# Second attention phase of a four-phase transformer kernel: regrouping DMAs two at a position, row transfers on ScalarE's queue

## The chip, the cores and the metric

The kernel runs on one core of a Trainium2 chip. The metric is the device time of one execution in microseconds (us), the median of several runs.

## What is computed

The input x (4 batches of 512 tokens, 512 features) goes through four residual blocks: causal attention with grouped keys and rotary embedding, a feed-forward block with 4-bit weights, causal attention with 32 heads and biases, and the feed-forward block again.

```python
x = x + _L0_attn_a_ref(_layernorm(x, axis=-1), ...)
x = x + _L0_ffn_ref(_layernorm(x, axis=-1), ...)
x = x + _L0_attn_b_ref(_layernorm(x, axis=-1), ...)
x = x + _L0_ffn_ref(_layernorm(x, axis=-1), ...)
```

The change touches the third block, which is

```python
q = (x @ Wq.T + bq).reshape(b, l, h, hd).transpose(0, 2, 1, 3)
...
scores = jnp.einsum('bhqd,bhkd->bhqk', q, k) / math.sqrt(hd)
...
att = jax.nn.softmax(scores, axis=-1)
out = jnp.einsum('bhqk,bhkd->bhqd', att, v)
out = out.transpose(0, 2, 1, 3).reshape(b, l, d)
return out @ Wo.T + bo
```

with h = 32 heads of hd = 16 and l = 512 tokens per batch.

## The kernel before, in words

The four phases run one after the other; tiles of the second attention phase have names that begin with `ab_`, those of the first with `aa_`. Each engine has its own instruction queue, written out by the same walk over positions; semaphores tie the queues together.

A batch is 16 pairs of heads, s = 0 to 15, and each pair has SUB = 5 positions, i = 0 to 4, so that a batch has positions 0 to 79. At every position TensorE makes one chunk of 512 columns of transposed scores (`exp_scores`, L1122), ScalarE takes its exponential (L834), GpSimd cuts off what lies above the diagonal (L691). Score banks alternate between two. At the same position TensorE makes score blocks of a pair two ahead, from which VectorE finds row maxima (`max_scores` L1082 and L1083, `reduce_max` L945 to L949). At i = 4 of an even pair the values matmuls (L1142) of the two pairs before follow.

The maximum is subtracted inside the score matmul: three more rows of the operand hold it, split into bf16 parts. For each pair they go from GpSimd's split through a transpose (L1106, i = 2 of the pair before) to VectorE's copy into `rowparts` (L958) and then by a DMA, the row transfer (L605), into the stacks. The first score chunk of a pair waits for it (`rows_made`).

The stacks hold Q and K of eight heads (a unit, four pairs) as rows of bf16 parts, in two buffers that alternate by unit. For each unit there is one projection of Q and one of K (tasks "Q" and "K", L247 with 12 matmuls and one for the bias). ScalarE, VectorE and GpSimd split the result into a high, middle and low part (`parted`, L810, L1024, L839, L716), and twelve DMAs of 128 KB, the sends, regroup them by head into the stacks (`regroup`, L652). The maxima of a unit's first pair wait for all twelve (`stacked`), and they begin two pairs ahead: unit u = 2 (pairs 8 to 11), for instance, is first read at position 30, in pair 6. The buffer that its sends overwrite is last read by the scores of position 19.

Other TensorE work stands at positions that a table, PLAN_B, sets: V (projection of values, positions 5 to 11), F and C (transposes of the context), O (output projection of the batch before, 14 to 17), X (transposes of the next batch's normalised x, 46, 48, 53, 56). Their results go through two task banks in PSUM. Q stands at 0, 20, 40 and 60, K two positions later, the last pair of them for the next batch. Only pairs 0 to 3 of the first batch and the end of the last run outside that rhythm: the last batch has no X and no Q and K for a next one.

Everything DMA in this phase is issued by SyncE, in order of position: the row transfer at i = 2, then the sends of Q and K two and three positions after their projection, loads of x, residuals, stores. The row transfer waits there for VectorE's copy, the sends for the parts:

```python
                        if i == ROWS_AT and (after := following(region, b0 + bs, s, 1)) is not None:
                            max_rows(*after)
                    for kind, bb, u, _ in table.started(region, pos, 2, "Q", "K"):
                        regroup(b0 + bb, u, QK.index(kind), (0,))
```

Of the kernel before, what the change touches and what calls it, by code (L numbers as in the profile page):

```python
# [250 lines left out]
class Timetable:  # L251
# [36 lines left out]
    def names(self, region):  # L288

        out = []  # L290
        for pos in range(len(region[0])):
            out += [(kind, u, t, 0) for kind, _, u, t in region[1].get(pos, []) if kind != "T"]
            out += [("T", u, t, p) for _, u, t, p in self.turned(region, pos)]
        return out
# [67 lines left out]
def attention(nc, phase, name, consts, x_dram, y_dram, w_dram, kv_heads, units, plan, head,  # L362
# [28 lines left out]
    with ExitStack() as ctx:  # L391
# [149 lines left out]
        SLOTS = (((0, 1, 2), (3, 4), (5,)), ((2, 4, 5), (0, 3), (1,)))  # L541
# [19 lines left out]
        block = ctx.enter_context(nc.Block())  # L561

# [8 lines left out]
        def _(sp):  # L571
# [29 lines left out]
            def max_rows(b, s):  # L601

                sp.wait_ge(rows_copied.sem, rows_copied.at(b, s + 1))
                h, _, _ = heads(s, 0)
                sp.dma_start(stacks[MAXROW:MAXROW + 3, unit(s) % 2, h:h + 2, :],  # L605
                             rowparts[MAXROW:MAXROW + 24, :]).then_inc(rows_made.sem, 16)

# [10 lines left out]
            def part(region, where, b0):  # L618
                for pos, step in enumerate(region[0]):
                    if step is not None:  # L620
                        bs, s, i = step
                        if i == ROWS_AT and (after := following(region, b0 + bs, s, 1)) is not None:
                            max_rows(*after)
                    for kind, bb, u, _ in table.started(region, pos, 2, "Q", "K"):
                        regroup(b0 + bb, u, QK.index(kind), (0,))
                    for kind, bb, u, _ in table.started(region, pos, 3, "Q", "K"):
                        regroup(b0 + bb, u, QK.index(kind), (1, 2))
# [14 lines left out]
                    if step is None and region is table.head and region[0][pos + 1] is not None:  # L642
                        max_rows(0, 0)

            def regroup(b, u, a, parts):

                for c in parts:
                    made, n = ((high_made, 1), (middle_made, 1), (lowest_made, 1))[c]
                    sp.wait_ge(made.sem, made.at(b, 2 * u + a + n))
                    for slot in SLOTS[a][c]:  # L650
                        first = HU if a else 0
                        sp.dma_start(stacks[slot * HD:(slot + 1) * HD, u % 2, first:first + HU, :],  # L652
                                     parted[:, a, c, :])\
                          .then_inc(regrouped[a].sem, 16)
# [90 lines left out]
        def _(act):  # L745
# [33 lines left out]
            def part(region, where, b0):  # L779
                for pos, step in enumerate(region[0]):  # L780
# [939 lines left out]
def late(first, step, kind):  # L1720
# [13 lines left out]
)  # L1734
PLAN_B = timed(
    *[(20 * (u - 1) + j, kind, 0, u, 0) for u in range(1, 4) for kind, j in (("Q", 0), ("K", 2))],
# [4 lines left out]
    *[(60 + j, kind, 1, 0, 0) for kind, j in (("Q", 0), ("K", 2))],  # L1741
# [75 lines left out]
```

## Time and profile before

| what | value |
|---|---|
| median of 3 runs | 1956.14 us (1955.39 to 1958.18) |
| the profiled execution | 1951.68 us, its span 1949.9 us |
| mean granted TensorE clock | 0.929 of full speed |
| busy: PE (TensorE), DVE (VectorE), ACT (ScalarE), POOL (GpSimd) | 1658.7, 1099.6, 861.1, 650.3 us |
| second attention phase, scores | from 987 to 1577 us of the span |

The span is cut by phase: the first attention phase ends near 576 us, the first feed-forward phase near 925 us. In a row of the timeline the first number is the start, the second the time until the last instruction of the row ended, and the bracket holds the engine's idle time before the row and what ended it. SPq is SyncE's queue; PEld is the weight load of TensorE.

### The profile page before, as it was taken

Reading aid. Unit: us, or ns where it says so; the run is one execution under the profiler, and the core shown is the slowest. Engines: PE = TensorE matmul, PEld = TensorE weight load, DVE = VectorE, ACT = ScalarE, POOL = GpSimd, SP = SyncE. Lnnn points to the kernel's source line nnn. Section 1 sums busy time; section 2 is a strip of 40 time slices with the busy share of each in tenths; the row PEclk is TensorE's granted clock in tenths of the full one; section 3 lists DMA queues with packets and bytes.
Section 4 is the critical chain, followed back from the end, with each engine's and each line's share of the span. In section 5 each row is a group of like instructions: output and inputs, shape, how many; then the busy total and the mean of one; then the engine's idle time right before and its main releaser. Section 6 shows DMA issues by size and latency. Waiting matters only on the chain. (4 is left out here: it accounts for less than half of the span.)

```text
span 1949.9 us, 31436 instructions
## 1 busy us (share of the span) xinstructions
PE 1658.7 (85%) x10544; PEld 1157.8 (59%) x10544; DVE 1099.6 (56%) x2394; ACT 861.1 (44%) x1514; POOL 650.3 (33%) x1926
## 2 busy tenths in 40 slices
PE   4888988989857999998288798798888857999997
PEld 4555655656535787786155475465555435777785
DVE  5777676676627654543555645644644527654543
ACT  3456555565524544532334433443443425454541
POOL 4455455454421221311224433433432412221211
PEclk8899999999997999999589898999889988999999
DMA  2000000001016311010534433633453226311010
GB/s 99 2 20 17 34 24 24 24 2 34 13 56 187 94 60 65 0 44 22 154 38 54 68 60 52 87 45 66 59 64 66 35 69 181 92 54 65 0 44 22
DMA packets 78118, 106.95 MB, mean 55 GB/s; under 512 B 13194, under 2 KB 49674, under 8 KB 77972
## 3 DMA queue, kind: packets, MB, share of 16 engines
q1 hardware_dynamic: 77972, 105.10, 24.1%
q8 instruction: 80, 1.31, 0.3%
q14 instruction: 66, 0.54, 0.1%
HBM read 62.34 MB, written 16.78 MB: 41 GB/s over the span
## 5 line engine op out<-in xcount | busy, mean ns | idle before, releaser
L247 PE MATMUL f_ring<-f_xt,f_codes 128*128 128x512 f32 (+1 forms) x1408 | 360.6, 399 | 6.6 <-DVEq L1539 5.5
L247 PEld LDWEIGHTS f_ring<-f_xt,f_codes 128*128 128x128 f32 (+1 forms) x1408 | 263.7, 188 | 76.0 <-DVEq L1539 6.2
L1397 POOL TENSOR_TENSOR f_ht<-f_work,f_ht 128x512 fp32r<-128x512 f32 (+1 forms) x88 | 114.6, 1306 | 472.9 <-ACT f_ht L1457 472.9
L834 ACT ACTIVATE ab_region<-ab_scores 128x512 f32<-128x512 f32 x320 | 181.0, 600 | 144.3 <-PE ab_scores L1122 144.2
L691 POOL TENSOR_SCALAR_AFFINE_SELECT ab_region<-ab_region 128x128 f32<-128x128 f32 x512 | 140.3, 298 | 240.5 <-ACT ab_region L834 240.2
L834 ACT ACTIVATE aa_region<-aa_scores 128x512 f32<-128x512 f32 x320 | 184.5, 599 | 81.3 <-PE aa_scores L1122 78.5
L1550 DVE TENSOR_TENSOR f_work<-f_ring,f_work 128x512 f32<-128x512 f32 (+1 forms) x176 | 120.6, 689 | 146.1 <-ACT f_work L1446 117.3
L1446 ACT ACTIVATE f_work<-f_ring,f_scales 128x512 f32<-128x512 f32 (+1 forms) x176 | 120.8, 686 | 171.7 <-PE f_ring L247 171.3
L1122 PE MATMUL ab_scores<-ab_stacks 99*128 99x512 bf16 (+3 forms) x512 | 135.4, 328 | 69.8 <-DMA ab_stacks<-ab_rowparts 66.8
L247 PE MATMUL f_ring<-f_dcodes,f_ht 128*128 128x512 f32 (+1 forms) x704 | 176.0, 404 | 10.3 <-DVE f_down_x L1520 9.3
L691 POOL TENSOR_SCALAR_AFFINE_SELECT aa_region<-aa_region 128x128 f32<-128x128 f32 x512 | 137.6, 299 | 88.5 <-ACT aa_region L834 88.0
L247 PEld LDWEIGHTS f_ring<-f_dcodes,f_ht 128*128 128x128 f32 (+1 forms) x704 | 133.0, 192 | 48.4 <-DVE f_down_x L1520 12.9
L1082 PE MATMUL aa_maxima<-aa_stacks 96*128 96x128 bf16 (+3 forms) x512 | 142.4, 312 | 21.4 <-DVE aa_nmax L949 15.6
L1082 PE MATMUL ab_maxima<-ab_stacks 96*128 96x128 bf16 (+3 forms) x512 | 147.6, 328 | 13.0 <-issue 12.6
L949 DVE TENSOR_REDUCE ab_nmax<-ab_maxima 128x1 f32<-128x384 f32 (+1 forms) x256 | 148.4, 616 | 17.6 <-PE ab_maxima L1083 14.9
L949 DVE TENSOR_REDUCE aa_nmax<-aa_maxima 128x1 f32<-128x384 f32 (+1 forms) x256 | 146.1, 614 | 2.7 <-PE aa_maxima L1083 1.0
L1122 PE MATMUL aa_scores<-aa_stacks 99*128 99x512 bf16 (+3 forms) x512 | 125.3, 306 | 7.2 <-DMA aa_stacks<-aa_rowparts 3.6
L1083 PE MATMUL ab_maxima<-mask_qk,identb 128*128 128x128 bf16 x512 | 115.4, 236 | 0.0
L1122 PEld LDWEIGHTS ab_scores<-ab_stacks 99*128 99x128 bf16 x512 | 45.6, 105 | 109.3 <-issue 84.7
L1083 PE MATMUL aa_maxima<-mask_qk,identb 128*128 128x128 bf16 x512 | 109.6, 226 | 0.0
L247 PE MATMUL ab_tasks<-ab_xt,ab_w 128*128 128x512 f32 x384 | 97.6, 403 | 7.0 <-DVE ab_bias L876 7.0
L945 DVE TENSOR_REDUCE ab_nmax<-ab_maxima 128x1 f32<-128x128 f32 x128 | 36.5, 285 | 117.1 <-PE ab_maxima L1083 117.1
(181 smaller groups left out, 2962.2 us busy)
## 6 DMA issues: line engine op xcount, KB each, us to landing
ab_stacks<-ab_parted SPq DMA_DIRECT2D x192, 128.0 KB, 5.6
f_x<-mid SPq DMA_DIRECT2D x32, 256.0 KB, 4.2
f_raw<-mid SPq DMA_DIRECT2D x32, 256.0 KB, 4.2
f_raw<-in_gate_q SPq DMA_DIRECT2D x10, 512.0 KB, 6.6
f_raw<-in_up_q SPq DMA_DIRECT2D x10, 512.0 KB, 4.9
f_raw<-in_down_q SPq DMA_DIRECT2D x10, 512.0 KB, 3.7
aa_x<-in_x SPq DMA_DIRECT2D x16, 256.0 KB, 2.8
aa_res<-in_x SPq DMA_DIRECT2D x16, 256.0 KB, 2.7
```

The source lines that it names most:

```text
L247: mm = pe.matmul(out, w, x, start=start and i == 0, stop=stop and i == len(pairs) - 1)
L691: last = pool.affine_select(out=chunk[:, at:at + P], in_=chunk[:, at:at + P], compare_op=ALU.is_ge, fill=0.0, base=0, pattern=[[1, P]], ch ...
L834: act.activation(probs[:, s // 2 % 2, SUB * (s % 2) + i, :], scores[:, sbk, :], ACT.Exp, scale=0.25).then_inc(scores_freed[sbk].sem, 1)
L945: dve.tensor_reduce(nm[:, h, 0:1], src[:, 0:P], AX_X, ALU.max, negate=True)
L949: last = dve.tensor_reduce(nm[:, h, qt:qt + 1], src[:, 0:(qt + 1) * P], AX_X, ALU.max, negate=True)
L1082: pe.matmul(out, lhs, rhs, start=True, stop=False, skip_group_check=True)
L1083: return pe.matmul(out[:, diag:diag + P], identb[:], mask[:], start=False, stop=True, skip_group_check=True)
L1122: mm = pe.matmul(scores[:, sbk, at:at + n], st[:, hk, kb * P:(kb + 1) * P], st[:, h, kb * P:T], start=True, stop=True)
L1397: pool.tensor_tensor(ht[0:r, LO, n, :], hid[0:r, n % 2, :], ht[0:r, HI, n, :].bitcast(F32), ALU.subtract).then_inc(hid_lo.sem, 1)
L1446: act.activation(scaled[0:r, j, :], src, ACT.Identity, scale=scales[0:r, j, n:n + 1])\
L1550: dve.tensor_tensor(dst, src, scaled[0:r, j, :], ALU.add)\
```

## The change

Three things change in the second attention phase; the first phase keeps its row transfers on SyncE (`if rope`).

1. The row transfer is issued by ScalarE's queue, behind the exponential of i = 3, the fourth of a pair.
2. The twelve sends of a unit are tasks of the plan ("S", numbers 0 to 11), two at a position: at positions 20, 21, 23, 24, 25 and 26 for unit 2, likewise from 40 and 60, and at 2, 3, 4, 5, 6 and 8 for unit 1. Ahead of the two, SyncE waits until the score chunk of the position before is made (`scores_seen`).
3. Q of units 2, 3 and of the next batch's unit 0 is projected at 17, 38 and 58 instead of 20, 40 and 60, K at 20, 40 and 60 instead of 22, 42 and 62.

```diff
+        SENDS = ((0, 0, 0), (0, 0, 1), (0, 0, 2), (0, 1, 3), (0, 1, 4), (1, 0, 2), (1, 0, 4), (1, 0, 5), (0, 2, 5),
+                 (1, 1, 0), (1, 1, 3), (1, 2, 1))
...
+        def max_rows(eng, b, s):
+
+            eng.wait_ge(rows_copied.sem, rows_copied.at(b, s + 1))
+            h, _, _ = heads(s, 0)
+            eng.dma_start(stacks[MAXROW:MAXROW + 3, unit(s) % 2, h:h + 2, :],
+                         rowparts[MAXROW:MAXROW + 24, :]).then_inc(rows_made.sem, 16)
...
-                        if i == ROWS_AT and (after := following(region, b0 + bs, s, 1)) is not None:
-                            max_rows(*after)
-                    for kind, bb, u, _ in table.started(region, pos, 2, "Q", "K"):
-                        regroup(b0 + bb, u, QK.index(kind), (0,))
-                    for kind, bb, u, _ in table.started(region, pos, 3, "Q", "K"):
-                        regroup(b0 + bb, u, QK.index(kind), (1, 2))
+                        if rope and i == ROWS_AT and (after := following(region, b0 + bs, s, 1)) is not None:
+                            max_rows(sp, *after)
...
+                    for n, (_, bb, u, t) in enumerate(table.started(region, pos, 0, "S")):
+                        if n == 0:
+                            scores_seen(b0 + bs, SUB * s + i - 1)
+                        regroup(b0 + bb, u, *SENDS[t])
...
+            def scores_seen(b, c):
+
+                sp.wait_ge(scores_filled[c % 2].sem, scores_filled[c % 2].at(b, c // 2 + 1))
+
+            def regroup(b, u, a, c, slot):
+
+                made = (high_made, middle_made, lowest_made)[c]
+                sp.wait_ge(made.sem, made.at(b, 2 * u + a + 1))
+                first = HU if a else 0
+                sp.dma_start(stacks[slot * HD:(slot + 1) * HD, u % 2, first:first + HU, :], parted[:, a, c, :])\
+                  .then_inc(regrouped[a].sem, 16)
...
                         act.activation(probs[:, s // 2 % 2, SUB * (s % 2) + i, :], scores[:, sbk, :], ACT.Exp,
                                        scale=0.25).then_inc(scores_freed[sbk].sem, 1)
+                        if not rope and i == ROWS_AT + 1 and (after := following(region, b, s, 1)) is not None:
+                            max_rows(act, *after)
...
+SENT = (0, 0, 1, 1, 3, 3, 4, 4, 5, 5, 6, 6)
```

SyncE's queue before, from pair 4 of the third batch on. A row with x12 is one unit's sends; rowparts rows are row transfers:

```order
L605 DMA ab_stacks<-ab_rowparts 3x8x128
L652 DMA ab_stacks<-ab_parted 16x8x512 x12
L605 DMA ab_stacks<-ab_rowparts 3x8x128 x4
L652 DMA ab_stacks<-ab_parted 16x8x512 x12
L605 DMA ab_stacks<-ab_rowparts 3x8x128
L578 DMA ab_x<-mid 128x512 x2
L605 DMA ab_stacks<-ab_rowparts 3x8x128 x3
L652 DMA ab_stacks<-ab_parted 16x8x512 x12
```

The same stretch of SyncE's queue in the changed kernel, from the last residual and stores ahead of it on:

```order
L612 DMA ab_res<-mid 128x512
L617 DMA mid<-ab_res 128x512
L612 DMA ab_res<-mid 128x512
L617 DMA mid<-ab_res 128x512
L660 DMA ab_stacks<-ab_parted 16x8x512 x24
L586 DMA ab_x<-mid 128x512 x2
L660 DMA ab_stacks<-ab_parted 16x8x512 x24
```

The row transfers are gone from it, and the sends of two units stand next to each other with nothing between them but their waits.

ScalarE's queue before, from pair 3 to pair 6 of the third batch. `ab_region<-ab_scores` is an exponential, `ab_parted` the casts of Q's and K's parts, `ab_avs` the copy of the context:

```order
L834 ACTIVATE ab_region<-ab_scores 128x512 x6
L810 CAST ab_parted<-ab_tasks 128x512
L834 ACTIVATE ab_region<-ab_scores 128x512 x2
L839 CAST ab_parted<-ab_rest 128x512
L810 CAST ab_parted<-ab_tasks 128x512
L834 ACTIVATE ab_region<-ab_scores 128x512 x2
L839 CAST ab_parted<-ab_rest 128x512
L777 COPY ab_avs<-ab_av 128x512
L834 ACTIVATE ab_region<-ab_scores 128x512 x9
L805 CAST ab_ct<-ab_tasks 128x512
L834 ACTIVATE ab_region<-ab_scores 128x512
```

And in the changed kernel, pairs 4 to 6 of the third batch:

```order
L841 ACTIVATE ab_region<-ab_scores 128x512
L817 CAST ab_parted<-ab_tasks 128x512
L841 ACTIVATE ab_region<-ab_scores 128x512 x2
L848 CAST ab_parted<-ab_rest 128x512
L841 ACTIVATE ab_region<-ab_scores 128x512
L568 DMA ab_stacks<-ab_rowparts 3x8x128
L841 ACTIVATE ab_region<-ab_scores 128x512
L784 COPY ab_avs<-ab_av 128x512
L841 ACTIVATE ab_region<-ab_scores 128x512 x4
L568 DMA ab_stacks<-ab_rowparts 3x8x128
L841 ACTIVATE ab_region<-ab_scores 128x512 x5
L568 DMA ab_stacks<-ab_rowparts 3x8x128
L812 CAST ab_ct<-ab_tasks 128x512
```

A row transfer stands behind each fourth exponential, ahead of the fifth; the casts keep their places behind the projections.

TensorE's queue before, from position 17 of pair 3 in the third batch to the end of that pair. The 12 matmuls from `ab_w,ab_ct` are O; `ab_scores` at 128x384 and 128x128 is the fourth chunk, at 128x256 x2 the fifth:

```order
L1150 MATMUL ab_tasks<-identf,ab_avs 128x128 x4
L247 MATMUL ab_tasks<-ab_w,ab_ct 128x512 x12
L247 MATMUL ab_tasks<-ab_bias,ab_sel 128x512
L1122 MATMUL ab_scores<-ab_stacks 128x384
L1122 MATMUL ab_scores<-ab_stacks 128x128
L1082 MATMUL ab_maxima<-ab_stacks 128x384
L1083 MATMUL ab_maxima<-mask_qk,identb 128x128
L1122 MATMUL ab_scores<-ab_stacks 128x256 x2
L1082 MATMUL ab_maxima<-ab_stacks 128x512
```

And in the changed kernel:

```order
L1159 MATMUL ab_tasks<-identf,ab_avs 128x128 x4
L247 MATMUL ab_tasks<-ab_w,ab_ct 128x512 x12
L247 MATMUL ab_tasks<-ab_bias,ab_sel 128x512
L247 MATMUL ab_tasks<-ab_xt,ab_w 128x512 x12
L247 MATMUL ab_tasks<-ab_sel,ab_bias_qk 128x512
L1131 MATMUL ab_scores<-ab_stacks 128x384
L1131 MATMUL ab_scores<-ab_stacks 128x128
L1091 MATMUL ab_maxima<-ab_stacks 128x384
L1092 MATMUL ab_maxima<-mask_qk,identb 128x128
L1131 MATMUL ab_scores<-ab_stacks 128x256 x2
```

The projection of Q (`ab_xt,ab_w`), which stood at position 20 behind this stretch, now stands behind O, ahead of the fourth chunk; behind the fourth chunk nothing but maxima and the fifth chunk is left in this pair.

## Rows read from the trace of the kernel before

**Rows 1.** Page: TensorE's busy time; the sends' size and time to landing.

```profile
PE 1658.7 (85%) x10544; PEld 1157.8 (59%) x10544; DVE 1099.6 (56%) x2394; ACT 861.1 (44%) x1514; POOL 650.3 (33%) x1926
...
ab_stacks<-ab_parted SPq DMA_DIRECT2D x192, 128.0 KB, 5.6
```

**Rows 2.** Windows, third batch and phase: busy us by engine, PEclk, DMA share, GB/s

```profile
1282.00:1436.00 154.00, 133.30 (x941) 86.47 (x942) 81.49 (x197) 63.08 (x116) 57.88 (x204) 0.91 0.42 60
...
sum 592.00, PE 507.25 PEld 325.16 DVE 308.54 ACT 248.02 POOL 226.44; mean PE 101.45 PEld 65.03 DVE 61.71 ACT 49.60 POOL 45.29
```

**Rows 3.** Waits of TensorE, 985 to 1577 us: total, times, longest.

```profile
PE ab_scores L1122 <- DMA ab_stacks<-ab_rowparts: 66.8, 24, 7.2
PE ab_tasks L1161 <- DVE ab_x L900: 10.5, 10, 2.1
```

**Rows 4.** Timeline of TensorE: first score chunks ahead of which it stood.

```profile
1079.40 0.58 PE L1122 MATMUL ab_scores<-ab_stacks 99*128 99x512 bf16 x1 [2.98 <-DMA ab_stacks<-ab_rowparts]
...
1232.56 0.58 PE L1122 MATMUL ab_scores<-ab_stacks 99*128 99x512 bf16 x1 [2.70 <-DMA ab_stacks<-ab_rowparts]
...
1269.18 0.58 PE L1122 MATMUL ab_scores<-ab_stacks 99*128 99x512 bf16 x1 [7.24 <-DMA ab_stacks<-ab_rowparts]
...
1353.66 0.59 PE L1122 MATMUL ab_scores<-ab_stacks 99*128 99x512 bf16 x1 [6.78 <-DMA ab_stacks<-ab_rowparts]
...
1387.31 0.58 PE L1122 MATMUL ab_scores<-ab_stacks 99*128 99x512 bf16 x1 [1.88 <-DMA ab_stacks<-ab_rowparts]
...
1540.80 0.58 PE L1122 MATMUL ab_scores<-ab_stacks 99*128 99x512 bf16 x1 [6.62 <-DMA ab_stacks<-ab_rowparts]
```

**Rows 5.** Timeline: SyncE's queue and VectorE's copy, pairs 4 and 5, third batch.

```profile
1338.37 7.76 SPq L652 DMA_DIRECT2D ab_stacks<-ab_parted  x12
...
1344.97 0.23 DVE L958 COPY ab_rowparts<-ab_av 24x128 bf16<-24x128 bf16 x1
...
1346.17 0.75 SPq L605 DMA_DIRECT2D ab_stacks<-ab_rowparts  x1
```

**Rows 6.** Line L652 from 1331 us (durations in ns); the window of their packets.

```profile
L652 SPq DMA_DIRECT2D ab_stacks<-ab_parted x12: 596/608/616, 1338.4 to 1345.5; - x12
...
1339.30:1352.20 12.90, 7.49 (x73) 3.88 (x71) 6.53 (x15) 5.33 (x10) 5.83 (x21) 0.94 1.04 123
```

**Rows 7.** Timeline: end of pair 7 of the third batch, start of pair 8.

```profile
1363.27 0.70 SPq L605 DMA_DIRECT2D ab_stacks<-ab_rowparts  x1
...
1363.55 0.38 PE L1122 MATMUL ab_scores<-ab_stacks 99*128 99x384 bf16 x2
...
1363.97 1.08 ACT L834 ACTIVATE ab_region<-ab_scores 128x512 f32<-128x512 f32 x2 [0.55 <-PE ab_scores L1122]
...
1364.71 0.22 PE L1083 MATMUL ab_maxima<-mask_qk,identb 128*128 128x128 bf16 x1
...
1365.30 0.38 PE L1122 MATMUL ab_scores<-ab_stacks 99*128 99x512 bf16 x1 [0.37 <-DMA ab_stacks<-ab_rowparts]
```

**Rows 8.** Timeline: pair 4 of the third batch.

```profile
1332.17 2.98 PE L247 MATMUL ab_tasks<-ab_xt,ab_w 128*128 128x512 f32 x12
...
1339.47 0.39 PE L1122 MATMUL ab_scores<-ab_stacks 99*128 99x384 bf16 x2
...
1340.15 1.09 ACT L834 ACTIVATE ab_region<-ab_scores 128x512 f32<-128x512 f32 x2
...
1343.08 0.39 PE L1122 MATMUL ab_scores<-ab_stacks 99*128 99x512 bf16 x1
```

**Rows 9.** Timeline: fourth chunk of pair 3, first chunk of pair 4, third batch.

```profile
1330.47 0.39 PE L1122 MATMUL ab_scores<-ab_stacks 99*128 99x384 bf16 x2
...
1331.70 0.38 PE L1122 MATMUL ab_scores<-ab_stacks 99*128 99x512 bf16 x1
```

**Rows 10.** Windows: the last of twelve stretches at half the clock, and their sum.

```profile
1565.70:1569.10 3.40, 3.40 (x16) 1.41 (x20) 0.92 (x2) 1.69 (x3) 2.19 (x9) 0.50 0.28 86
sum 92.40, PE 60.49 PEld 36.45 DVE 36.30 ACT 31.45 POOL 24.85; mean PE 5.04 PEld 3.04 DVE 3.02 ACT 2.62 POOL 2.07
```

More of the change, by code:

```diff
@@ L291, in names @@
         for pos in range(len(region[0])):
-            out += [(kind, u, t, 0) for kind, _, u, t in region[1].get(pos, []) if kind != "T"]
+            out += [(kind, u, t, 0) for kind, _, u, t in region[1].get(pos, []) if kind not in "TS"]
             out += [("T", u, t, p) for _, u, t, p in self.turned(region, pos)]
@@ L538, in attention @@
         OTHER_W = [max(head_at("P")) + 2 + 2 * f for f in range(KD)] if rope else [12, 13, 15, 16]
-        SLOTS = (((0, 1, 2), (3, 4), (5,)), ((2, 4, 5), (0, 3), (1,)))
+        SENDS = ((0, 0, 0), (0, 0, 1), (0, 0, 2), (0, 1, 3), (0, 1, 4), (1, 0, 2), (1, 0, 4), (1, 0, 5), (0, 2, 5),
+                 (1, 1, 0), (1, 1, 3), (1, 2, 1))
         FIRST = sum(len(ks) for ahead, ks in MAXIMA_AT if ahead == 2)
@@ L599, in _ @@
                 load(1, t)
[L601 to L606, printed above, removed]
             def residual(b, t):
@@ L621, in part @@
                         bs, s, i = step
-                        if i == ROWS_AT and (after := following(region, b0 + bs, s, 1)) is not None:
-                            max_rows(*after)
-                    for kind, bb, u, _ in table.started(region, pos, 2, "Q", "K"):
-                        regroup(b0 + bb, u, QK.index(kind), (0,))
-                    for kind, bb, u, _ in table.started(region, pos, 3, "Q", "K"):
-                        regroup(b0 + bb, u, QK.index(kind), (1, 2))
+                        if rope and i == ROWS_AT and (after := following(region, b0 + bs, s, 1)) is not None:
+                            max_rows(sp, *after)
+                    if step is None and region is table.head:
+                        for kind, bb, u, _ in table.started(region, pos, 2, "Q", "K"):
+                            for a, c, slot in SENDS:
+                                if a == QK.index(kind):
+                                    regroup(b0 + bb, u, a, c, slot)
+                    for n, (_, bb, u, t) in enumerate(table.started(region, pos, 0, "S")):
+                        if n == 0:
+                            scores_seen(b0 + bs, SUB * s + i - 1)
+                        regroup(b0 + bb, u, *SENDS[t])
                     for _, bb, _, t in table.started(region, pos, 2, "X"):
@@ L642, in part @@
                     if step is None and region is table.head and region[0][pos + 1] is not None:
[L643 to L654, printed above, removed]
+                        max_rows(sp, 0, 0)
+            def scores_seen(b, c):
[6 more added lines that the diff above has]
+                  .then_inc(regrouped[a].sem, 16)
             whole(sp, part)
@@ L1734 @@
 )
+SENT = (0, 0, 1, 1, 3, 3, 4, 4, 5, 5, 6, 6)
 PLAN_B = timed(
-    *[(20 * (u - 1) + j, kind, 0, u, 0) for u in range(1, 4) for kind, j in (("Q", 0), ("K", 2))],
+    (0, "Q", 0, 1, 0), (2, "K", 0, 1, 0),
+    *[(j, "S", 0, 1, n) for n, j in enumerate((2, 2, 3, 3, 4, 4, 5, 5, 6, 6, 8, 8))],
+    *[(20 * (u - 1) + j, "S", 0, u, n) for u in (2, 3) for n, j in enumerate(SENT)],
     *[(j, "V", 0, 0, t) for t, j in enumerate((5, 7, 9, 11))],
@@ L1740 @@
     *[(j, "X", 1, 0, t) for t, j in enumerate((46, 48, 53, 56))],
-    *[(60 + j, kind, 1, 0, 0) for kind, j in (("Q", 0), ("K", 2))],
+    (17, "Q", 0, 2, 0), (20, "K", 0, 2, 0), (38, "Q", 0, 3, 0), (40, "K", 0, 3, 0),
+    (58, "Q", 1, 0, 0), (60, "K", 1, 0, 0),
+    *[(60 + j, "S", 1, 0, n) for n, j in enumerate(SENT)],
 )
```

## The prediction

> **What bounds the kernel now.** I read the page first, to see which engine is full in the phase that the diff touches. TensorE is busy 85% of the span [rows 1]. Then I cut the second attention phase into its batches: in the third TensorE is busy 133.3 of 154 us (87%) at a mean granted clock of 0.91, VectorE, the next in busy time, 81.5 us (53%) [rows 2]. So what can be won is TensorE's idle time and its slow stretches. The waits of TensorE in this phase say who ends the idle time: 66.8 us in 24 waits end with the row transfer (ab_rowparts to ab_stacks); the next item, waits for the normalised x, is 10.5 us [rows 3].
>
> The 24 are of two kinds. Below, T4 is the start of pair 4's first score matmul, counted within a batch; positions run from 0 (pair 0, i=0) to 79. Seven long waits stand ahead of pair 6 (all batches) and pair 14 (not in the last batch, which regroups nothing there); one of 6.78 and the longest, 7.24, are shown. Four stand ahead of pair 10: 2.98, 2.70, 1.88 and 6.62 us, 14.2 together [rows 4]. Thirteen of about 0.37 us (4.8 together) stand ahead of pairs that follow a pair without a task behind its third score chunk, like the one ahead of 1365.30 [rows 7]. The seven are then 66.8 - 14.2 - 4.8 = 47.8 us.
>
> Why 6.8 us? SyncE's own queue tells it: twelve regrouping DMAs (third batch, pair 4 on) hold the queue from 1338.37 to 1346.13, and pair 6's row transfer starts only at 1346.17, though VectorE's copy was ready at 1345.20 [rows 5]. It then stands behind twelve times 128 KB [rows 1, 5]. During 12.9 us the DMA engines are full (share 1.04), so one regrouping DMA costs 12.9/12 = 1.07 us of them [rows 6]. TensorE resumes at 1353.66 [rows 4], 1.4 us after their end and 7.5 us after the row transfer's issue, where an undisturbed row transfer takes 2.03 us: issued 1363.27, next pair begins 1365.30 [rows 7].
>
> Removing the row wait alone would therefore give nothing: pair 6's first maxima need the regrouped stacks (the wait in `stacked`), which land at that same time. What counts is when the twelve sends land, and how much TensorE work lies before.
>
> **The change, part by part.** Times are against the profiled execution (1951.68 us, span 1949.9), which is 4.5 us under the median of 1956.14; I apply the difference to both.
>
> *Projections earlier, sends from position 20, 40, 60.* The projection of Q for the next unit moves from position 20 to 17 (40 to 38, 60 to 58), and K from 22 to 20. Work is the same: a projection is 2.98 us of matmuls and one for the bias, together about 3.1 us of TensorE [rows 8]. Before, pair 6 began 22.0 us after T4 (1331.70 [rows 9] to 1353.66). Afterwards pair 4 holds one projection less: 11.4 us (1331.70 to 1343.08 [rows 8]) - 3.1 = 8.3. Pair 5 has 3.8 us of work (1343.08 to the start of the wait, 1353.66 - 6.78 = 1346.88). So pair 6 could begin at T4 + 12.1. The sends: four go out at once (T4 to T4+2.5, 0.61 us of queue each [rows 6]); the next need the scores of positions 22 to 25, which follow K, so two each from T4+4.4, 5.4 and 6.0, and the last pair at T5+0.4 = T4+8.7, ending its issue near T4+10. Eight DMAs from T4+5.4 on keep the DMA engines to about T4+13.9, plus 1.4 for the tail as above: landed at T4+15.3. TensorE still does pair 6's first score chunk (0.2), then waits with the maxima: 15.3 - 12.1 - 0.2 = 3.0 us, at pair 14 likewise. Gain: 47.8 - 7 x 3.0 = 26.8 us. In the last batch pair 9 holds no transposes of x, and pair 10 behaves like pair 6: 6.62 - 3.0 = 3.6. In the first three batches pair 9 is long (about 8.7 us), the sends land before pair 10, and 2.98 + 2.70 + 1.88 = 7.6 is gained; the waits for normalised x (10.5 us in ten [rows 3]) stay. Sum of this part: 38.0 us.
>
> Q at positions 38 and 58 stands behind the fourth score chunk, so it also covers the row transfer of the short pairs 7 and 11: seven waits of 0.36 like that of [rows 7], 2.5 us gained. Moving K and Q past F, O and X costs nothing in work; the two task banks must be free for F, O and Q at position 17, but O's 3.1 us lie between F and Q.
>
> *Row transfer behind the fourth exponential, on ScalarE.* This is the price. VectorE's copy is at i=2; SyncE issued at once. In the short pair 7 the fourth chunk of scores starts at 1363.55, its exponential at 1363.97 and ends at about 1364.5, and TensorE could begin the next pair at 1364.93 [rows 7]. So the issue comes 0.7 to 1.3 us later than 1363.27, depending on whether ScalarE's queue issues while the exponential runs or after it. No DMA of ScalarE is in this trace. I take the later end and the 2.03 us measured on SyncE's queue: issue 1.05 after the chunk, 3.1 to the next pair, where 1.38 is work (1363.55 to 1364.93): a pause of 1.7 us instead of 0.37. Who pays: the short pairs without Q, V, X or values behind the fourth chunk. Pair 15 into the next batch (3 x 1.3 = 3.9). Pair 3, where the exponential also waits for the cast of Q now made at position 17: in the present trace such an exponential starts 0.68 instead of 0.42 after its chunk (1339.47 to 1340.15 [rows 8]). There the next pair starts 1.23 after the chunk today (1330.47 to 1331.70 [rows 9]) and would start at 3.3: 2.1 us, in four batches, less the 0.4 already paid in the first: 8.0. In the last batch pairs 11 and 13 (no Q): 2.6. Pairs 5, 9 of the last batch and 13 pay it inside the pause computed above. Sum: 14.5 us lost.
>
> Even pairs end with the values matmuls: from fourth chunk to next pair they need 3.6 us (1339.47 to 1343.08 [rows 8]) against 3.1, so they just hide it. But pairs 0 and 8 now have sends in flight at that moment; their packets share the DMA engines. Bounds: nothing, if the small packets slip between, to 1 us; I take 0.5 in eight cases, 4 us (pairs 4 and 12 absorb it in the later pause).
>
> The 0.70 us that the DMA takes on the issuing queue [rows 7] now falls on ScalarE, 63 times, 44 us, beside 248 us of work in the phase's 592 [rows 2]. It delays the fifth exponential, needed only by the second chunk of the next pair, which starts 0.5 us after the late first: covered. Without that cover it would be 0.7 us a pair.
>
> The Trainium skill (DMA: Bandwidth & Descriptors, Issuing engines are not separate DMA queues) says that DMAs of any engine run on the same 16 DMA engines, and issuing from several saves only the issue time. By that alone, a second queue would not shorten the wait behind sends; the full share in [rows 6] agrees that the engines are the shared resource. The same page (Queues, rings and completion order) has each DMA engine alternate between the queues that have work, which would let a small transfer slip in; no row here shows either. What the first reading would cost is rival 2, worked out from rows.
>
> *Clock.* After each long pause TensorE's granted clock is 0.5, the 1.2 GHz level, and a score matmul takes 0.58 [rows 4] instead of 0.38 us [rows 7]. Over the phase I count twelve such stretches, 60.5 us of TensorE busy in them [rows 10], so about 30 us are lost to half speed, 2.5 each. Shorter pauses may remove some; the nine new ones of 1.7 to 2.1 may each bring one like that at 1565.7, 3.4 us busy [rows 10], 1.7 lost, 15 in all. I take zero, with -15 and +30 as bounds.
>
> **Sum:** 38.0 + 2.5 - 14.5 - 4 = 22.0 us faster: 1929.7 for a profiled run, 1934 for the median.
>
> **Rivals.**
> 1. *The slow stretches go* as well, because no pause exceeds 3 us. For: a 0.37 us pause never has one behind it. Against: the pauses at pair 10 are 1.9 to 3 and have one. Half to two thirds of the 30: about 1916. Chance 0.20.
> 2. *Slower: row transfers still stand behind the sends.* Pair 4's rows are issued at T4+6.2 with about three sends' worth of backlog; if they wait for it, pair 5 begins at T4+10.7 instead of 8.3. In fifteen regroupings that is 15 x 2.4 = 36 us, 32 over what is counted: 1934 + 32 = 1966. It decides the sign from (22 + 4)/15 = 1.7 us a regrouping on. For: pair 6's 7.5 us today. Against: that was one queue, in order. Chance 0.07.
> 3. *A DMA on ScalarE's queue costs about 0.9 us more to land*: then four even pairs a batch and the short ones are exposed by it, about 25 times 0.9, which eats the 22: 1956, no change. Nothing in the trace shows or excludes it. Chance 0.08.
> 4. *The new pauses each bring a slow stretch*: 15 us back, 1949. Chance 0.15.
> 5. The forecast: 1926 to 1942, chance 0.50.
>
> The range runs from 1912 to 1955. What a measurement can tell from no change is 0.2%, 4 us. Cases 1, 4 and 5 give 0.85 for faster, of which I move 0.02 for misjudged tails: faster 0.83, same 0.07, slower 0.10.
>
> **What would show it.** Right: waits of scores for the row transfer ahead of pair 6 gone, and a wait of maxima on the regrouped stacks of about 3 us in its place; row waits of 1.5 to 2 us ahead of pairs 4 and 0; none ahead of pairs 8 and 12; ScalarE's row transfer starting as the fourth exponential ends. The step that I trust least is landing at T4+15.3: two us either way are 16 us in the sum. It would be wrong altogether if the row transfer lands later than 3 us after issue in most pairs, or if slow stretches of the clock grow in number.

## The result: about 10 us faster, where 22 were forecast

The changed kernel takes 1948.6 us (median of 10 runs, 1942.78 to 1952.22); the kernel before, run beside it, 1958.32 us (10 runs, 1955.39 to 1963.33). The ratio is 0.9946, 95% interval [0.9934, 0.9959]: faster by 0.4 to 0.7%. The profiled execution took 1948.8 us, its span is 1947.0 us, the mean granted clock 0.935.

The page of the changed kernel, TensorE's row and that of the sends (issue to landing in the last number, 4.1 us where [rows 1] has 5.6):

```profile
PE 1669.1 (86%) x10544; PEld 1159.5 (60%) x10544; DVE 1099.4 (56%) x2394; ACT 864.5 (44%) x1514; POOL 647.5 (33%) x1926
...
ab_stacks<-ab_parted SPq DMA_DIRECT2D x192, 128.0 KB, 4.1
```

From the first score of the phase to the first of its last pair the kernel before needed 583.26 us and the changed one 574.36, so the phase is 8.9 us shorter. The spans of the two traces differ by only 2.9 us, because outside the phase, where the change has next to nothing to act on, this trace of the kernel before is the quickest of all (1366.6 us against 1372.6, and 1370.0 to 1377.4 in the runs below). A difference of phases is therefore read from one trace each: run 8, which takes as long as the changed kernel, has a phase 2.7 us shorter. What TensorE waited for from 985 to 1577 us (total, times, longest), to be read against [rows 3]:

```profile
PE ab_scores L1131 <- DMA ab_stacks<-ab_rowparts: 45.5, 33, 3.3
PE ab_tasks L1170 <- DVE ab_x L909: 10.6, 9, 2.1
PE ab_av L1115 <- POOL ab_nparts L688: 6.2, 4, 2.3
PE ab_maxima L1091 <- DVE ab_nmax L958: 4.4, 11, 0.4
PE ab_maxima L1091 <- DVE ab_nmax L955: 3.6, 7, 0.5
```

The row waits fell from 66.8 to 45.5 us, 21.3 less. The third to fifth row show what ate almost half of that. Before, waits for GpSimd's parts were 1.6 us and those of maxima for VectorE 0.4 us. Now they are 3.9 and 8.1, 10.1 more. (The 6.2 of the third row hold one of 2.3 us ahead of the phase's first score; the kernel before has the same one, just outside the window.)

The row waits have also moved. By pair, over the four batches:

| wait ahead of pair | before, us each | changed, us each |
|---|---|---|
| 0 | 0.4 | 1.1 |
| 1 | 0 | 3.3 in the first batch, then 1.0 |
| 4 | 0.4 in the first batch, then 0 | 1.1 |
| 5 | 0 | 1.2 |
| 6 | 6.8 to 6.9 | 1.7 to 1.8 |
| 8 and 12 | 0.3 to 0.4 | 0 (12 in the last batch: 1.1) |
| 9 | 0 | 1.7 to 1.8 (0.8 in the first batch) |
| 10 | 3.0, 2.7, 1.9, 6.6 | 0.5, 0, 0.5, 2.7 |
| 13 | 0 | 0.6, 1.7, 0, 0 |
| 14 | 6.4 to 7.2 (0.4 in the last batch) | 1.3 to 2.7 (1.1 in the last batch) |

Two pairs of the third batch show how it goes. First the timeline from the fourth chunk of pair 3 (where [rows 9] stood), then that of pair 4's own transfer. ACTq is ScalarE's queue, SPq SyncE's; L568 is the row transfer:

```profile
1332.15 0.39 PE L1131 MATMUL ab_scores<-ab_stacks 99*128 99x384 bf16 x2
...
1332.59 0.73 ACTq L568 DMA_DIRECT2D ab_stacks<-ab_rowparts  x1
...
1332.83 1.14 ACT L841 ACTIVATE ab_region<-ab_scores 128x512 f32<-128x512 f32 x2
...
1333.02 13.71 SPq L660 DMA_DIRECT2D ab_stacks<-ab_parted  x12
...
1334.68 0.38 PE L1131 MATMUL ab_scores<-ab_stacks 99*128 99x512 bf16 x1 [1.14 <-DMA ab_stacks<-ab_rowparts]
...
1340.36 0.23 DVE L967 COPY ab_rowparts<-ab_av 24x128 bf16<-24x128 bf16 x1
1340.39 0.62 ACT L841 ACTIVATE ab_region<-ab_scores 128x512 f32<-128x512 f32 x1
...
1340.62 0.73 ACTq L568 DMA_DIRECT2D ab_stacks<-ab_rowparts  x1
...
1341.23 0.39 PE L1091 MATMUL ab_maxima<-ab_stacks 96*128 96x512 bf16 x1 [0.40 <-DVE ab_nmax L958]
...
1345.13 0.38 PE L1131 MATMUL ab_scores<-ab_stacks 99*128 99x512 bf16 x1 [1.17 <-DMA ab_stacks<-ab_rowparts]
```

Three things are to be seen. The issue at 1332.59 comes before the fourth exponential starts (1332.83), and the one at 1340.62 in the middle of one that lasts until 1341.01: ScalarE's queue issues the DMA without waiting for that exponential to end. With no send ahead of it the transfer takes 2.09 us (1332.59 to 1334.68), as on SyncE's queue [rows 7]. With sends in flight it takes 4.51 us (1340.62 to 1345.13), and TensorE stands 1.17 us ahead of pair 5.

The windows of pairs 4, 5 and 6 of that batch (length; busy us of PE, PEld, DVE, ACT and POOL with their instructions; PEclk, DMA share, GB/s):

```profile
1334.68:1345.13 10.45, 8.88 (x70) 4.84 (x71) 4.98 (x12) 4.36 (x8) 6.18 (x20) 1.00 0.65 111
1345.13:1350.39 5.26, 3.60 (x29) 2.27 (x30) 4.19 (x11) 2.87 (x5) 1.74 (x7) 1.00 0.53 75
1350.39:1357.81 7.42, 7.42 (x61) 3.98 (x62) 4.38 (x10) 3.36 (x6) 3.15 (x14) 0.77 0.00 1
```

Pairs 4 and 5 now take 15.7 us, where T4+15.3 was forecast: the end is nearly right, but it is reached in another way. Pair 4 takes 10.45 instead of 8.3 us, and the pause ahead of pair 6 is 1.7 instead of 3.0. The DMA engines are idle in pair 6: the sends had landed by then, and no maxima wait on them. In pairs 8 and 9 the pause that goes (the one ahead of pair 10) was only 1.9 to 3.0 us long in the first three batches [rows 4], and the slower pairs 8 and 9 eat more than that: over the four batches they lose 2.8 us, with the projection that left pair 8 put back. Pair 8 takes 11.6 us in the third batch:

```profile
1370.80 0.39 PE L1091 MATMUL ab_maxima<-ab_stacks 96*128 96x512 bf16 x1 [0.52 <-DVE ab_nmax L955]
...
1371.03 0.73 ACTq L568 DMA_DIRECT2D ab_stacks<-ab_rowparts  x1
...
1371.65 0.39 PE L1091 MATMUL ab_maxima<-ab_stacks 96*128 96x512 bf16 x1 [0.40 <-DVE ab_nmax L958]
...
1376.08 0.38 PE L1131 MATMUL ab_scores<-ab_stacks 99*128 99x512 bf16 x1 [1.71 <-DMA ab_stacks<-ab_rowparts]
```

That is 0.92 us of waits for VectorE within the pair and 1.71 behind a row transfer that took 5.05 us.

### The profile page after: what moved, and what is told of

Its sections match the earlier page's. It is cut to its first block and busy times, and to the rows that moved or that the text cites. A ratio compares the mean times of both kernels' runs of the same rounds, so it can differ in the third digit from the quotient of the medians.

```text
span 1947.0 us, 31527 instructions
## 1 busy us (share of the span) xinstructions
PE 1669.1 (86%) x10544; PEld 1159.5 (60%) x10544; DVE 1099.4 (56%) x2394; ACT 864.5 (44%) x1514; POOL 647.5 (33%) x1926
## 3 DMA queue, kind: packets, MB, share of 16 engines
q8 instruction: 80, 1.31, 0.3%
## 5 line engine op out<-in xcount | busy, mean ns | idle before, releaser
L1131 PE MATMUL ab_scores<-ab_stacks 99*128 99x512 bf16 (+3 forms) x512 | 130.1, 318 | 47.8 <-DMA ab_stacks<-ab_rowparts 45.5
```

The lines of the kernel that those rows point to most:

```text
L1131: mm = pe.matmul(scores[:, sbk, at:at + n], st[:, hk, kb * P:(kb + 1) * P], st[:, h, kb * P:T], start=True, stop=True)
```

## Experiments

All times are medians, all ratios are against the kernel before on the same chip. "Phase" is the time from its first score to the first score of its last pair, 583.3 us before and 574.4 with the whole change.

**1. The row transfers alone.** The kernel before, with only this part of the change.

```diff
-                        if i == ROWS_AT and (after := following(region, b0 + bs, s, 1)) is not None:
-                            max_rows(*after)
+                        if rope and i == ROWS_AT and (after := following(region, b0 + bs, s, 1)) is not None:
+                            max_rows(sp, *after)
...
+                        if not rope and i == ROWS_AT + 1 and (after := following(region, b, s, 1)) is not None:
+                            max_rows(act, *after)
```

> Kernel before, with the row transfers alone moved to ScalarE's queue behind the fourth exponential. My theory: the long pauses ahead of pairs 6 and 14 come from the sends' landing, which stays where it was, so they stay at 6 us or more, now as a wait of the maxima on the stacks; the short pairs pay about 0.75 us more each (1.1 instead of 0.38). Not faster: 1956 to 1970 us. Rival, that the row transfer's own queue is what the change gains by: the long pauses go and the time is within 5 us of the changed kernel's 1948.6.

Measured: 1960.06 us, ratio 1.0007 [0.9988, 1.0025], phase 590.6. Row waits, and the third batch from pair 4 (T4 = 1346.03) to pair 6:

```profile
PE ab_scores L1124 <- DMA ab_stacks<-ab_rowparts: 66.9, 39, 4.3
```
```profile
1350.36 8.22 SPq L652 DMA_DIRECT2D ab_stacks<-ab_parted  x12
...
1354.24 0.73 ACTq L567 DMA_DIRECT2D ab_stacks<-ab_rowparts  x1
...
1359.57 0.38 PE L1124 MATMUL ab_scores<-ab_stacks 99*128 99x512 bf16 x1 [2.09 <-DMA ab_stacks<-ab_rowparts]
...
1365.82 0.38 PE L1124 MATMUL ab_scores<-ab_stacks 99*128 99x512 bf16 x1 [2.65 <-DMA ab_stacks<-ab_rowparts]
```

The time is the expected one, the mechanism is not. The total of the waits is the same to 0.1 us, in 39 pieces instead of 24. The pauses of 6 us and more are gone (at most 2.7 ahead of 6 and 14) although projections and sends stand where they stood. One reason is that the sends start at T4+4.3 instead of T4+6.7 (1331.70 to 1338.37 [rows 5, 9]): SyncE no longer waits for VectorE's copy ahead of them. The last one lands at T4+19.5 instead of T4+22.0, by the semaphore events of the two traces, and in both pair 6's rows land within 0.2 us of it. The other reason is that pairs 4 and 5 have become longer (the wait ahead of pair 5 alone is 2.1 us), so less of that time is left as a pause. What is won there is lost ahead of pairs 1, 5, 9 and 13 (1.9 to 2.1 us each, 4.3 ahead of pair 1 of the first batch; 5.33 us from issue to score above) and of pairs 0, 4, 8 and 12 (1.1 to 1.3 each).

**2. The sends and projections alone.** The changed kernel with its row transfers back on SyncE, at the third chunk.

```diff
-                        if rope and i == ROWS_AT and (after := following(region, b0 + bs, s, 1)) is not None:
+                        if i == ROWS_AT and (after := following(region, b0 + bs, s, 1)) is not None:
...
-                        if not rope and i == ROWS_AT + 1 and (after := following(region, b, s, 1)) is not None:
-                            max_rows(act, *after)
```

> Changed kernel, with the row transfers back on SyncE's queue at i=2; sends and projections as in the change. My theory: the earlier and spread sends carry the gain, and the row transfer on SyncE is issued 0.9 us earlier than on ScalarE, so the pauses of 1.13 us ahead of pairs 0 and 4 fall to 0.4 or nothing, those ahead of pairs 5, 9 and 13 fall too; ahead of pair 6 it waits for all sends, 3 us. 1938 to 1946 us. Rival, own queue needed: row transfers stand behind sends, the pauses ahead of 5, 6, 9, 13, 14 are over 3 us each and the time is 1955 or more.

Measured: 1952.80 us, ratio 0.9970 [0.9954, 0.9986], phase 577.3: a miss, by 7 us. The timeline of pairs 4 to 6 of the third batch (T4 = 1336.49):

```profile
1343.82 5.12 SPq L660 DMA_DIRECT2D ab_stacks<-ab_parted  x8
...
1348.13 0.23 DVE L965 COPY ab_rowparts<-ab_av 24x128 bf16<-24x128 bf16 x1
...
1348.98 0.75 SPq L568 DMA_DIRECT2D ab_stacks<-ab_rowparts  x1
...
1355.02 0.58 PE L1129 MATMUL ab_scores<-ab_stacks 99*128 99x512 bf16 x1 [4.98 <-DMA ab_stacks<-ab_rowparts]
```

On SyncE the rows of pair 4 hold back eight of the sends until the copy is made (1342.96), and pair 6's rows then stand behind those eight. The pauses ahead of 6 and 14 are 4.9 to 5.1 us. Nothing waits ahead of pairs 5, 9 and 13, and yet pair 4 takes 9.73 us and pairs 8 and 12 take 9.80, not 8.3.

**3. The whole change, one chunk earlier.** The row transfer on ScalarE, behind the third exponential.

```diff
-                        if not rope and i == ROWS_AT + 1 and (after := following(region, b, s, 1)) is not None:
+                        if not rope and i == ROWS_AT and (after := following(region, b, s, 1)) is not None:
```

> Changed kernel, with ScalarE issuing the row transfer behind the third exponential of a pair instead of the fourth. My theory: each row transfer starts about 0.7 us earlier; the pauses ahead of pairs 0 and 4 fall from 1.13 to about 0.4, those ahead of 1, 5, 9, 13 by 0.7 each: 33 waits of 45.5 us in all shrink to some 25, 1930 to 1942 us. Rival: ScalarE's queue now stands for VectorE's copy and holds up the fourth exponential, which delays the scores; no gain, 1946 to 1952.

Measured: 1934.95 us, ratio 0.9880 [0.9855, 0.9905], phase 559.6. Row waits, and pair 4's transfer of the third batch:

```profile
PE ab_scores L1131 <- DMA ab_stacks<-ab_rowparts: 30.6, 23, 2.8
```
```profile
1331.20 0.73 ACTq L568 DMA_DIRECT2D ab_stacks<-ab_rowparts  x1
...
1335.73 0.38 PE L1131 MATMUL ab_scores<-ab_stacks 99*128 99x512 bf16 x1 [1.19 <-DMA ab_stacks<-ab_rowparts]
```

The chunk is worth 14 us, as expected. Ahead of pairs 1 and 4 the waits are all but gone; ahead of 5 they are not (1.2 us in three of four batches), since there VectorE's copy is what the issue waits for, and the transfer takes 4.53 us among the sends.

**4. K two positions later.** The changed kernel with K at 22, 42 and 62, and the sends that need it one position later.

```diff
-SENT = (0, 0, 1, 1, 3, 3, 4, 4, 5, 5, 6, 6)
+SENT = (0, 0, 1, 1, 3, 4, 4, 5, 5, 6, 6, 7)
...
-    (17, "Q", 0, 2, 0), (20, "K", 0, 2, 0), (38, "Q", 0, 3, 0), (40, "K", 0, 3, 0),
-    (58, "Q", 1, 0, 0), (60, "K", 1, 0, 0),
+    (17, "Q", 0, 2, 0), (22, "K", 0, 2, 0), (38, "Q", 0, 3, 0), (42, "K", 0, 3, 0),
+    (58, "Q", 1, 0, 0), (62, "K", 1, 0, 0),
```

> Changed kernel, with K projected at positions 22, 42 and 62 as before the change (Q stays at 17, 38, 58), and its sends up to one position later. My theory: K at position 20 leaves short positions behind it in which TensorE waits for VectorE's reductions (8.0 us in 18 waits of the maxima); these go, while the last sends land later and the pause ahead of pairs 6 and 14 grows by 1 to 2 us: 1942 to 1950 us. Rival: those waits would only turn into row waits, the time stays or gets worse, 1948 to 1956, because the row transfer and not VectorE is late in these pairs.

Measured: 1966.03 us, ratio 1.0030 [1.0012, 1.0049], phase 594.1: a miss, slower than the kernel before.

```profile
PE ab_scores L1131 <- DMA ab_stacks<-ab_rowparts: 47.7, 23, 4.9
PE ab_av L1115 <- POOL ab_nparts L688: 17.6, 15, 2.3
```

K's matmuls do cover the row transfer (no waits ahead of 5, 9 and 13), but the pauses ahead of 6 and 14 are 3.6 to 3.9 us, and the waits for GpSimd's parts grow from 6.2 to 17.6 us (both with the 2.3 us from ahead of the first score). The clock has a part in it too: 18 stretches at half clock instead of 12, with 69.5 us of TensorE busy in them instead of 54.2, which costs 7.7 us.

**5. A gap around the row transfer.** Seven of the twelve sends wait for position 26 (46, 66). The sends of unit 1, which lie around pair 1's transfer, stay.

```diff
-SENT = (0, 0, 1, 1, 3, 3, 4, 4, 5, 5, 6, 6)
+SENT = (0, 0, 1, 1, 1, 6, 6, 6, 6, 6, 6, 6)
```

> Changed kernel, with five sends of Q at positions 20 and 21 and the seven others held back to position 26 (in pair 5), so that no send is in flight when pair 5's row transfer goes out. Theory A, sends in flight make the row transfer late (4.5 instead of 2.1 us to land): the pauses ahead of pairs 5, 9 and 13, 1.1 to 1.8 us in the changed kernel, vanish; the sends land later, so the pause at pair 6 and 14 grows to 3 us or more. Time 1950 to 1962. Theory B, these pauses come from the row transfer's late issue (VectorE's copy is late) and not from sends: they stay at 1 us or more.

Measured: 1984.12 us, ratio 1.0130 [1.0111, 1.0148]. The time missed by over 20 us; the mechanism that the run was made for showed. By the semaphore events the row transfers ahead of pairs 5, 9 and 13 now land 1.9 to 2.0 us after their issue, where the changed kernel has up to 5.0, and nothing waits ahead of these pairs: pair 4 takes 9.2 us and pairs 8 and 12 take 9.8. Ahead of pair 1 the waits stay (1.0 to 1.1 us, 3.4 in the first batch). The late sends are paid further on:

```profile
PE ab_scores L1131 <- DMA ab_stacks<-ab_rowparts: 61.9, 22, 5.1
PE ab_maxima L1091 <- DMA ab_stacks<-ab_parted: 11.9, 8, 3.5
```

**6. No pacing.** The sends in bursts, as soon as their parts are made.

```diff
-SENT = (0, 0, 1, 1, 3, 3, 4, 4, 5, 5, 6, 6)
+SENT = (0, 0, 0, 0, 0, 1, 1, 1, 1, 2, 2, 2)
```

> Changed kernel, with the sends as early as their parts are there (five at position 20, four at 21, three at 22, behind the same waits for the parts) instead of two at a position. In the changed kernel the last two sends wait for pair 5's first scores and go out 10.9 to 12.7 us after pair 4's start. Theory A, the pacing costs: the last send goes out about 9.5 us after pair 4's start, the pauses ahead of 6 and 14 (1.3 to 2.7 us) go to 1 or less, those ahead of 5, 9, 13 grow by up to 1 us: 1942 to 1948. Theory B, the pacing protects the row transfers: those ahead of 5, 9 and 13 grow to over 3 us and the time is 1952 or more.

Measured: 1944.69 us, ratio 0.9923 [0.9903, 0.9944]. The waits ahead of 9 and 13 grow to 1.5 to 3.0 us, those ahead of 6 and 14 are 0.2 to 1.8. The time is the one expected if pacing costs, but the interval overlaps that of the change (up to 0.9944 against from 0.9934). So no gain from two at a position can be seen; a cost of some 4 us is likely and not shown.

**7. Bursts, and rows behind the third exponential** (the edits of 3 and 6 together).

> As e6_burst, and the row transfer behind the third exponential, as in e3_rows_third (1935 us). If pacing costs nothing and saves nothing, 1935 again; under theory A of e6_burst 1928 to 1934, under theory B 1938 or more.

Measured: 1930.41 us, ratio 0.9858 [0.9835, 0.9882], phase 560.4. Against run 3 (1934.95 us, phase 559.6) the intervals overlap again and the phase is no shorter, so this run doesn't settle what pacing costs.

**8. ScalarE's queue doubled.** The changed kernel with a second small DMA behind each row transfer.

```diff
+                            act.dma_start(dummy[0:24, :], identb[0:24, :]).then_inc(dummy_made, 16)
```

> Changed kernel, and behind each row transfer ScalarE issues a second DMA of the same size from a constant to a tile that nothing reads (63 times 0.73 us more on ScalarE's queue ahead of the fifth exponential). My theory: the queue time on ScalarE is covered, within 5 us of the changed kernel (1948.6). Rival: the fifth exponential's delay reaches TensorE through the two score banks, and each 0.73 us costs about as much in the short pairs: 1960 or more, and then the first 0.73 us of the change itself cost as much.

Measured: 1949.59 us, ratio 0.9952 [0.9938, 0.9967], row waits 44.4 us in 33. The timeline behind pair 4's rows:

```profile
1338.83 0.76 ACTq L569 DMA_DIRECT2D ab_stacks<-ab_rowparts  x1
1339.63 0.76 ACTq L848 DMA_DIRECT2D ab_dummy<-identb  x1
1340.43 0.60 ACT L842 ACTIVATE ab_region<-ab_scores 128x512 f32<-128x512 f32 x1 [1.21 <-issue]
```

The fifth exponential is 0.8 us later, 63 times, and the time doesn't move: the queue time on ScalarE is covered, as the prediction had it.

**9. Short reductions.** Run 2 with less work for VectorE: in the second phase the reductions with more than 256 columns read only the first 128. This leaves out part of the maxima, so the run is read for its time alone.

```diff
-                    last = dve.tensor_reduce(nm[:, h, qt:qt + 1], src[:, 0:(qt + 1) * P], AX_X, ALU.max,
+                    last = dve.tensor_reduce(nm[:, h, qt:qt + 1], src[:, 0:(qt + 1) * P if rope else P], AX_X, ALU.max,
```

> The changed kernel with its row transfers back on SyncE at the third score (as in the run with the sends alone), and VectorE's reductions of the second phase, from the third half of a score on, over only the first 128 columns: this leaves out part of the maxima, so the output is not the reference's and its time is read for one thing alone. Theory: pairs 4, 8 and 12 take 9.7 to 9.8 us in the run with the sends alone, though no row wait stands behind them, because VectorE with K's rest and the reductions is late; with short reductions they take 8.3 to 8.9 us and most of the 8 us in which maxima wait for VectorE's negated maxima goes. Rival: VectorE is not what is late there, and they stay at 9.6 to 9.8 us.

Measured: 1939.65 us, ratio 0.9899 [0.9872, 0.9927], phase 566.3. The waits of maxima for VectorE (9.8 us in run 2) are gone from the list, and so are those for GpSimd's parts (2.7 us in run 2 behind the first score). Pair 4 takes 9.2 us and pairs 8 and 12 take 8.94: half a microsecond and 0.86 less than in run 2. So VectorE is over a third of what pair 4 and over half of what pairs 8 and 12 have over 8.3 us. In pair 4, 0.9 us stays over 8.3, of which TensorE is idle for only 0.23; its cause is open. VectorE was 53% busy in the phase (312.4 of 592 us); taking 77 us from it was worth 13 us to 1952.8.

**10. K one position later.** Run 7 with K at 21, 41 and 61.

```diff
-    (17, "Q", 0, 2, 0), (20, "K", 0, 2, 0), (38, "Q", 0, 3, 0), (40, "K", 0, 3, 0),
-    (58, "Q", 1, 0, 0), (60, "K", 1, 0, 0),
+    (17, "Q", 0, 2, 0), (21, "K", 0, 2, 0), (38, "Q", 0, 3, 0), (41, "K", 0, 3, 0),
+    (58, "Q", 1, 0, 0), (61, "K", 1, 0, 0),
```

> The changed kernel with its sends in bursts and its row transfers behind the third exponential (1930.4 us so far, as an earlier run gave it), and K's projections at 21, 41 and 61 instead of 20, 40 and 60: VectorE's copy of the rows of the following pair then comes before K's rest, and K's matmuls lie inside pair 4's row transfer. Theory that the late copy costs what is left ahead of pairs 5, 9 and 13: those waits fall by 0.5 us each or more and the time is 1920 to 1930 us. Rival: as with K two positions later, what is won there comes back as waits for GpSimd's parts and as later sends, and the time is 1932 to 1945 us.

Measured: 1926.43 us, ratio 0.9824 [0.9800, 0.9847], phase 555.5.

```profile
PE ab_scores L1131 <- DMA ab_stacks<-ab_rowparts: 24.1, 14, 3.4
```
```profile
1340.08 0.73 ACTq L568 DMA_DIRECT2D ab_stacks<-ab_rowparts  x1
...
1344.34 0.59 PE L1131 MATMUL ab_scores<-ab_stacks 99*128 99x512 bf16 x1 [2.60 <-DMA ab_stacks<-ab_rowparts]
```

The waits ahead of 5, 9 and 13 are gone, and pair 4 with K in it takes 9.4 us. Pauses of 2.3 to 2.8 us stand again ahead of 6 and 14. This is the fastest kernel of the study, 22 us under the change; against run 7 the intervals overlap. The waits ahead of 5, 9 and 13 did go, and the phase is shorter (560.4 to 555.5), but that is one trace each, so the size of the step is not shown.

## Why the prediction was half right

**Direction right, size not.** 22 us were forecast against a measured 9.7, and the phase of the trace moved by 8.9. That 1948.6 lies in the range of 1912 to 1955 is no merit of the sum: it is within 1 us of what rival 4 gives, and rival 4 didn't happen. The following goes through the sum by pairs, from the starts of the pairs' first chunks in the two traces, with 3.05 us (a projection, from the first of its matmuls at 1332.17 [rows 8] to the score chunk behind it at 1335.22) put back for every Q that changed its pair.

| pairs | forecast, us | traces, us |
|---|---|---|
| 4 and 5 (with the pause ahead of 6) | +15.4 | +13.0 |
| 12 and 13 (with the pause ahead of 14) | +10.1 | +8.8 |
| 8 and 9 | +9.2 | -2.8 |
| 3 | -8.0 | -4.1 |
| 0 to 2 | -2.0 | -8.9 |
| 14 and 15 | -3.9 | +2.7 |
| 6 and 7 | +1.4 | +5.6 |
| 10 and 11 | -0.2 | -5.3 |
| sum | +22.0 | +8.9 |

**The step that failed: what a row transfer and the work beside it cost while sends are in flight.** The prediction had even pairs "just hide" their transfer, put 0.5 us on pairs 0 and 8, and let pairs 4 and 12 absorb it. The waits ahead of pairs 1, 5, 9 and 13 come to 19.4 us in the trace (6.3 + 4.8 + 6.0 + 2.3), against 4. Run 5 shows the cause for 13.1 of them by taking it away: with the sends out of the way the waits ahead of 5, 9 and 13 are zero. For pair 1, whose sends run 5 leaves alone, run 2 says the same: there its rows are issued with no send in flight, and no wait stands ahead of it. That is the mechanism of rival 2, which was given 7 in 100: pair 5 begins at T4+10.45 and rival 2 said 10.7. The agreement is part luck, since only 1.17 us of it is a wait and the rest is the second error. The rival's price of 36 us was too high: the pairs' own work, longer than 8.3 us, covers part of the transfer, and what pairs 4 and 12 lose comes off the pause that follows. In pairs 0 and 8 it is a loss in full. Most of what is missing lies there: rows "0 to 2" and "8 and 9" of the table are 18.9 us short of the forecast, other rows give some of it back. In the first batch pair 1 also runs into a stretch at half clock behind its wait of 3.3 us and takes 15.2 us instead of 13.1.

**"Costs nothing in work"** was the second error, and belongs to the same pairs. Subtracting 3.1 us from pair 4's 11.4 took it that TensorE was the only thing in those 11.4. Without row waits the pairs take 9.2 to 9.8 us (runs 2 and 5). With one projection less, the maxima follow each other closer than VectorE reduces them: K's rest (0.69 us) and the copy stand in its queue as well. Run 9 ties 0.5 to 0.86 us of each such pair to VectorE. Together with the waits for GpSimd's parts ahead of L1115 in pair 10 of the first three batches, these new waits are 10.1 us. The latter are VectorE's as well: GpSimd starts on the parts only when VectorE's last reduction has ended,

```profile
1386.34 0.19 POOL L681 CAST ab_nparts<-ab_nmax 128x8 bf16<-128x8 f32 x1 [2.38 <-DVE ab_nmax L958]
```

and in run 9, with short reductions, they are gone.

**Pauses ahead of 6 and 14.** Forecast 3.0, measured 1.3 to 2.7; the forecast's place of the wait was wrong, as it is still the row transfer and not the maxima on the stacks. But the row transfer lands within 0.2 us of the last send in all seven, so the landing of the sends, which the prediction trusted least, is what sets the end of the pause, and it was right: T4+15.7 in the third batch against T4+15.3. Part of what looks like gain here is the second error over again: pair 4 had become longer. The sentence "Removing the row wait alone would therefore give nothing" gave the right time for run 1 and the wrong reason. It left out that SyncE's wait for the copy delayed the sends.

**Row transfer behind the fourth exponential.** Forecast 1.7 to 2.1 us ahead of pairs 0 and 4, measured 1.1: the DMA is issued 0.4 to 0.5 us after its chunk and not 1.05. All in all this term was 14.5, and the exposures ahead of 0, 4, 12 (last batch) and 14 (last batch) cost 7.8 over what stood there before. The landing time was right (2.09 us against 2.03), which rules out rival 3.

**Pairs 8 and 12.** As forecast no wait stands ahead of them in the first three batches; Q at 38 and 58 covers the transfer.

**Queue time of ScalarE.** Right; run 8.

**Clock.** Before and after, twelve stretches at half clock, with 60.5 and 54.2 us of TensorE busy in them; at 1.2 instead of 2.4 GHz that difference is 3 us. So rival 1 didn't happen (they did not go), nor did rival 4. Behind the sixteen waits of 0.9 to 1.25 us ahead of scores no slow stretch begins within 2.5 us. Behind those of 1.6 us and more it often does (eight of twelve have one that begins in the wait or within 2.5 us behind it): the window of pair 6 above has a PEclk of 0.77 after a wait of 1.66 us, and pair 10 of the same batch has one of 0.71, with two waits of 1.31 us (for GpSimd's parts) and 0.84 us (for x) in it:

```profile
1384.76:1396.48 11.72, 9.57 (x66) 4.45 (x66) 8.53 (x21) 3.95 (x7) 5.25 (x20) 0.71 0.10 26
```

That pair alone, 8.48 us before and 11.72 now, is 3.2 of the 5.3 us lost in pairs 10 and 11.

**The page cited.** The prediction set one rule of the Trainium skill (DMA: Bandwidth & Descriptors, Issuing engines are not separate DMA queues) against another (the same page, Queues, rings and completion order). From issue to score a row transfer takes 6.0 us (run 2) and 7.5 us [rows 4, 5] on the queue of the sends, and 4.5 to 5.3 us on its own queue in the rows above. That looks like a gain of the second queue, and it isn't one: fewer sends were in flight. Counted over all row transfers of a trace, with landings by the semaphore events (median us from issue to landing, lowest to highest):

| sends in flight at the issue | on SyncE's queue, with the sends | on ScalarE's queue |
|---|---|---|
| 0 | 1.9 (kernel before) | 1.9 (changed kernel) |
| 4 | 4.1, 2.7 to 4.3 (run 2) | 4.2, 3.5 to 5.0 (changed kernel) |
| 6 | 5.9, 5.0 to 6.0 (run 2) | 5.9, 4.7 to 6.2 (run 6) |
| 7 | 7.4, 5.5 to 7.8 (kernel before) | none |

So the traces agree with the first rule, and no shorter landing by the alternation of the second is seen in them. What the second queue changed is the order and the time of the issues: SyncE's sends no longer wait for the copy (run 1), and the rows are issued with fewer sends ahead of them.

## What to carry to other kernels

A pause that falls from 7 to 2 us is worth only what the work ahead of it doesn't take back: when a stage loses TensorE work, look at what its other engines do per pair before counting the whole difference, even where they are half idle on average. A small transfer on the path should not be issued while a burst is in flight, on whatever queue: here it landed as late on its own queue as on that of the burst. A queue of its own is of use where the two would hold up each other's issue. Where the transfer can't be kept out of the burst, issue it as early as its data allow (one chunk was worth 14 us here); matmuls behind it that need nothing from it cover it (K in runs 4 and 10), but moving them has its own price, as run 4 shows. Moving the waiting DMA off the queue of the burst and moving the burst earlier gave 0 and 6 us alone, 10 together, and 24 with the issue a chunk earlier; the pacing gave nothing that these runs could see.

## What the hardware showed that was not expected

ScalarE's queue issues a DMA before the ACTIVATE ahead of it has run: at 1332.59, while that exponential starts at 1332.83. The DMA holds the queue for 0.73 us.

A row transfer of 24 rows of 256 bytes takes 2.09 us from issue to score alone and 4.5 to 5.3 us beside 128 KB sends of another queue (4.51, 5.05, 5.33, 4.53 in the rows above). How long it takes goes by the number of sends in flight and not by the queue: 5.9 us to landing with six of them on either.
